# The pooled side one chunk ahead of the weighted sum, in the second weighted stage of a four-layer graph network

## The chip, the cores and the metric

The kernel runs on one core of one Trainium2 chip. The metric is the device time of one execution in microseconds. The kernel before took 19959.1 us (median of 3 runs, 19957.56 to 19962.43).

## The reference

Four residual graph layers over 12500 nodes with 64 features and 412500 directed edges, sorted by their target node. Each layer normalises x, applies a relu and adds one message passing step:

```python
h = jnp.maximum(_layernorm(x, axis=-1), 0.0)
x = x + _L0_gnn_ref(h, edge_weight1, src, dst, L0_gnn_W, L0_gnn_b)       # segment_sum(h[src] * e, dst) @ W.T + b
h = jnp.maximum(_layernorm(x, axis=-1), 0.0)
x = x + _L1_gnn_ref(h, edge_index, edge_attr_32, u, batch0, W1, b1, W2, b2)
h = jnp.maximum(_layernorm(x, axis=-1), 0.0)
x = x + _L2_gnn_ref(h, L2_gnn_weight_r, src, dst, edge_type_8)           # a relational layer over 8 types
h = jnp.maximum(_layernorm(x, axis=-1), 0.0)
x = x + _L3_gnn_ref(h, L3_gnn_attn_l, L3_gnn_attn_r, src, dst)           # a softmax attention layer

# inside _L1_gnn_ref, by source node (row = edge_index[0]):
seg_sum = jax.ops.segment_sum(edge_attr, row, num_segments=N)
seg_max = jax.ops.segment_max(edge_attr, row, num_segments=N)
cnt = jax.ops.segment_sum(jnp.ones((edge_attr.shape[0], 1)), row, num_segments=N)
h = jnp.concatenate([seg_sum, seg_max, seg_sum / jnp.maximum(cnt, 1.0), u[batch]], axis=1)
return jax.nn.relu(h @ W1 + b1) @ W2 + b2
```

The change touches the stage that computes the last two thirds of the weighted sum of layer 0 and, beside it, the sums and maxima of the edge features of layer 1 (the "pooled" work) and the count of edges per target node.

## The kernel before

**Tiling.** The edges are laid out as 128 partitions of J = 3224 edges. A chunk is L = 60 edges of every partition; there are 54. A segment sum is a running scan along each partition's edges with a link (0 or 1) that restarts it where the node changes; the scans are stored to HBM, and later one row per node, the last of its run, is fetched back.

**Stages, in order.** `gathered_layer("wsum", 0 .. 18)` (66 to 1825 us in the profile), `scatter_by_source`, which sorts the edge features by source node into `by_src` (to 7065), `gathered_layer("wsum", 18 .. 54, pooled=True)`, which is changed (to 10022), `first_layers`, which turns the fetched rows into the output of layers 0 and 1 (to 10479), then the relation gathers (to 14981), its update, the attention gathers (15291 to 19814) and its update. Between stages all engines meet at a barrier. The function `gathered_layer` is shared by all four gathered stages; what the change adds is bound to `pooled`, and `pooled` is true for this stage alone.

**The stage that is changed.** NC = 36 chunks, and for each chunk k three pieces of work on DVE:

- own(k), lines 555 to 618: waits for the chunk's gathered rows of h (`gathered`), multiplies them by the edge weights (line 580, which says `turned`) and scans them (line 616, `scanned`).
- count_side(k), lines 461 to 479: makes one-hots of 90 target indices (fewer in the last side) in HG = 3 groups of HL = 30, a `low` (line 478) and a `high` (line 479), in NB = 3 pairs of buffers. For each group it waits for `oh_used`, that is, for PE to have read what lies in the buffer; PE multiplies high by low, 30 matmuls a group (line 786), and so counts the edges per node.
- pool_side(k), lines 481 to 517: waits for 90 sorted rows (`prow_loaded`), for ACT to have turned them (`pturned`) and taken the side before (`ptaken`), and runs a sum scan and a max scan over them (line 511), which ends with `pscanned`.

The sides have 90 edges where a chunk has 60: the 36 sides cover all 54 chunks' edges, the 36 chunks only the last two thirds.

Around them:

- POOL, lines 430 to 446, gathers chunk k's rows of h, 60 indirect DMAs (line 437; 44 for the last chunk). Chunks 0 and 1 of the stage were gathered earlier. Before each chunk it waits for `index_ready` (ACT has copied the chunk's indices), `turned` (own(k-2) has used up the buffer) and `oh_used` (the count sides up to three before are on PE). Ahead of this it has the scatters of the sort, line 881. Behind the last gather it waits until all pooled scans are stored (line 453), and issues the first EARLY = 28 fetches of their rows (line 1066); first_layers issues the others.
- ACT, lines 689 to 757, for each k: `number_following(k)` (line 712) copies the indices of chunk k+2, once chunk k's rows have landed; `turn_pooled(k)` (line 692) turns the sorted rows of side k; own(k) (lines 737 and 739) turns and stores the chunk's scan; `take_pooled(k)` (lines 701 and 703) turns and stores the pooled scans in two halves through one buffer, so the second half waits until the first is stored.
- SP, lines 410 to 421: `load_rows(k)` loads the sorted rows of side k once side k-1 has been scanned (line 413); the first waits for the end of the scatters.

The order on each engine is the order in which the code is written; loops run over pairs of chunks with i = k // 2 and s = k % 2. DVE before: own, count, pool for k = 0 to 33, then own(34), pool(34), count(34), pool(35), count(35), own(35).

Of the kernel before, what the change touches and what calls it, by code (L numbers as in the profile page):

```python
# [43 lines left out]
def build(nc, x, src, dst, etype, weight, attr, W0, b0, u, W1, b1, W2, b2, Wr, attn_l, attn_r, out, L):  # L44
# [39 lines left out]
    with ctx:  # L84
# [204 lines left out]
        def gathered_layer(kind, table, width, rows_out, c0, c1, index, counts=None, pooled=False, weights=None,  # L289
# [5 lines left out]
            NC = c1 - c0  # L295
            SIDE = JP // NC
            SHORT = SIDE - (JP - J)
# [3 lines left out]
            CHUNKS = NC + (1 if REST else 0)  # L301
            rest_at = (NC - 1) * L + FINAL
            HG = SIDE // HL
            NB = HG
            BY, PBY = 512 // L, 512 // SIDE
            with ExitStack() as c:
# [151 lines left out]
                def _(dve):  # L458
# [158 lines left out]
                                                            ALU.mult, ALU.add)  # L617
                            last.then_inc(scanned, 1)

                    def side(i, s):  # L620

                        if counts:
                            count_side(i, s)
                        if pooled:
                            pool_side(i, s)

                    with dve.Fori(0, NC // 2 - 1) as i:
                        for s in range(2):
                            own(i, s)
                            side(i, s)  # L630
                    own(NC // 2 - 1, 0)
                    for s in range(2):
                        if pooled:
                            pool_side(NC // 2 - 1, s, SHORT if s else SIDE)
                        if counts:
                            count_side(NC // 2 - 1, s, SHORT if s else SIDE)
                    own(NC // 2 - 1, 1, FINAL)
# [36 lines left out]
                def _(act):  # L674
# [14 lines left out]
                    def turn_pooled(k, w=SIDE):  # L689

                        act.wait_ge(prow_loaded, 32 * k + 32)
                        nc.scalar.copy(by_feature_of(flat_of(pGf), A, w), prow[:, 1:w + 1, 0:A].rearrange("p j f -> p f j")).then_inc(pturned, 1)

                    def take_pooled(k, w=SIDE):

                        run = by_feature_of(flat_of(pSf), 2 * A, w)
                        act.wait_ge(pscanned, k + 2)
                        for half in range(2):
                            act.wait_ge(pstored, 32 * k + 16 * half + 16)
                            rows = slice(half * w // 2, (half + 1) * w // 2)  # L700
                            nc.scalar.copy(pS[:, 0:w // 2, :].rearrange("p j f -> p f j"), run[:, :, rows]).then_inc(ptaken, 1)  # L701
                            act.wait_ge(ptaken, 2 * k + half + 2)
                            act.dma_start(scan_pool[0:EP, :].rearrange("(p j) f -> p j f", p=P)[:, bass.ds(k * SIDE + half * w // 2, w // 2), :],
                                          pS[:, 0:w // 2, :]).then_inc(pstored, 16)
# [9 lines left out]
                    def own(i, s, w=L, following=True, at=None):  # L714
# [19 lines left out]
                            else:  # L734
# [3 lines left out]
                            act.wait_ge(taken_out, k + 2)  # L738
                            act.dma_start(rows_out[0:EP, :].rearrange("(p j) f -> p j f", p=P)[:, bass.ds(at, w), :],
                                          S[s][:, 0:w, :]).then_inc(stored[s], 16)  # L740
                    def own_and_pooled(i, s):

                        if pooled:
                            number_following(i, s)
                            turn_pooled(2 * i + s)
                        own(i, s)
                        if pooled:
                            take_pooled(2 * i + s)

                    with act.Fori(0, NC // 2 - 1) as i:  # L750
                        own_and_pooled(i, 0)
                        own_and_pooled(i, 1)
                    own_and_pooled(NC // 2 - 1, 0)
                    if pooled:
                        turn_pooled(NC - 1, SHORT)
                        take_pooled(NC - 1, SHORT)
                    own(NC // 2 - 1, 1, FINAL, False)
                    if REST:
                        own(NC // 2, 0, REST, False, rest_at)
# [891 lines left out]
        def attention_update():  # L1651
            with ExitStack() as c:  # L1652
# [61 lines left out]
                def _(sp):  # L1714
# [6 lines left out]
                    if N > full * P:  # L1721
# [9 lines left out]
                       pooled=True, weights=wt_all, carried=wsum_state)  # L1731
# [58 lines left out]
```

## Time and profile before

| | |
|---|---|
| median of 3 runs | 19959.1 us |
| profiled execution | 19961.19 us, its span 19959.5 us |
| POOL busy | 13577.9 us (68%) |
| DVE busy | 8460.5 us (42%) |
| ACT busy | 2726.7 us (14%) |
| PE busy | 2311.4 us (12%) |
| second weighted stage | 7065 to 10022 us |
| first_layers | 10022 to 10479 us |

The numbers come from one profiled execution. A line's busy time is the time in which its instructions were running on the engine; for an indirect DMA of POOL it is the time to issue it, not to carry it out. "Idle before" is the time for which the engine stood still ahead of an instruction, with what released it. "Issue" as a releaser means that nothing in the profile explains the pause. In a timeline ACTq and SPq are the issue of a transfer from that engine's queue. `wsum_C` is the count in PSUM, `lead_rows` the gathered rows, `H` in this stage the pooled scans, `wsum_idx` the indices that POOL reads, `taken` and `scan_wsum` belong to the correction that joins the partitions' runs in first_layers.

### The profile page before, as it was taken

What the parts mean: (1) busy time and instruction counts of PE and PEld (TensorE: products, weight loads), DVE (VectorE), ACT (ScalarE), POOL (GpSimd) and SP (SyncE); (2) the same over time, 40 slices, a digit from 0 to 9 for tenths busy, and PEclk for the clock granted to TensorE, in tenths of its full rate; (3) what the DMA queues carried; (4) which work ended last, traced back from release to release, by engine and by line L of the source; (5) the groups of instructions that cost most, each with busy time, mean ns of one, the idle gap of its engine ahead of it and who ended that gap; (6) DMA issues with size and microseconds to landing.
All of it is one profiled execution on the core that took longest, in us unless ns stands there. A gap on an engine that the chain in (4) does not pass through costs nothing. (4 is left out here: it accounts for less than half of the span.)

```text
span 19959.5 us, 67952 instructions
## 1 busy us (share of the span) xinstructions
PE 2311.4 (12%) x17213; PEld 2000.1 (10%) x17213; DVE 8460.5 (42%) x6902; ACT 2726.7 (14%) x1877; POOL 13577.9 (68%) x13406
## 2 busy tenths in 40 slices
PE   1112222222222211111140000000000000000000
PEld 1111222222222200000030000000000000000000
DVE  6666667766666666666631111111113222222222
ACT  0000010000100022222221111111110100111110
POOL 5665556665566666666637777777776777777776
PEclk7555555555555555555565555555555555555555
DMA  3111111111111122223321111111112111111111
GB/s 66 45 41 53 50 50 50 54 54 50 50 50 50 48 93 97 98 95 101 108 83 44 47 47 47 47 47 47 47 49 31 48 48 48 48 48 48 48 48 48
DMA packets 611147, 1134.47 MB, mean 57 GB/s; under 512 B 329487, under 2 KB 381168, under 8 KB 569104
## 3 DMA queue, kind: packets, MB, share of 16 engines
q0 software_dynamic: 428736, 387.04, 9.6%
q10 hardware_dynamic: 33984, 425.89, 5.2%
q1 hardware_dynamic: 148368, 320.87, 4.9%
q8 instruction: 22, 0.36, 0.0%
q14 instruction: 37, 0.30, 0.0%
HBM read 613.19 MB, written 519.73 MB: 57 GB/s over the span
## 5 line engine op out<-in xcount | busy, mean ns | idle before, releaser
L881 POOL DMA_INDIRECT by_src<-H,sort_place_i x3224 | 3131.1, 971 | 2047.9 <-DVE sort_place_i L949 1080.8
L437 POOL DMA_INDIRECT rel_G<-rel_table,rel_idx x3224 | 3457.0, 1072 | 1239.3 <-issue 1029.5
L437 POOL DMA_INDIRECT att_G<-att_table,att_idx x3224 | 3429.5, 1064 | 1057.9 <-issue 1057.9
L437 POOL DMA_INDIRECT lead_rows<-h_table,wsum_idx x3104 | 2948.5, 950 | 1581.8 <-issue 934.6
L610 DVE SCALAR_TENSOR_TENSOR rel_Gf<-rel_Sf,rel_keep_first,rel_Gf 128x64 f32<-128x64 f32 x55 | 18.5, 336 | 3964.7 <-ACT rel_Gf L729 2065.8
L584 DVE TENSOR_TENSOR_SCAN att_near<-att_near,er_in 128x60 f32<-128x60 f32 (+2 forms) x55 | 19.3, 351 | 3435.9 <-DMA att_G<-att_table,att_idx 3435.9
L1038 PE MATMUL pG<-sort_cnt,sort_lowT 128*128 128x98 f32 x6448 | 1273.8, 361 | 885.8 <-DVE sort_prod L935 819.5
L478 DVE TENSOR_TENSOR wsum_low<-iota_b,wsum_parts 128x3840 fp8e4<-128x3840 bf16 x216 | 891.8, 4129 | 1080.5 <-remote 881.4
L1038 PEld LDWEIGHTS pG<-sort_cnt,sort_lowT 128*128 128x128 f32 x6448 | 1155.7, 268 | 894.6 <-DVE sort_prod L935 827.5
L786 PE MATMUL wsum_C<-wsum_high,wsum_low 128*128 128x98 fp8e4 x6448 | 720.6, 267 | 3963.3 <-issue 3272.1
L935 DVE TENSOR_TENSOR sort_prod<-pG,sort_high 128x392 f32<-128x392 f32 x806 | 450.9, 565 | 1605.5 <-remote 1209.9
L989 ACT COPY sort_cnt<-pC 128x392 f32<-128x392 f32 x806 | 391.8, 486 | 4695.3 <-PE pC L1030 2300.9
L786 PEld LDWEIGHTS wsum_C<-wsum_high,wsum_low 128*128 128x128 fp8e4 x6448 | 526.0, 131 | 4158.0 <-issue 4157.6
L729 ACT COPY rel_Gf<-rel_G 128x3840 f32<-128x3840 f32 (+2 forms) x55 | 358.1, 6511 | 3293.6 <-DMA rel_G<-rel_table,rel_idx 3293.6
L928 DVE TENSOR_REDUCE sort_rank<-sort_keys 128x60 f32<-128x7680 int16 (+1 forms) x54 | 784.2, 14523 | 1.9
L920 DVE TENSOR_TENSOR sort_lowT<-sort_lows,sort_side 128x7680 f32<-128x7680 uint8 (+1 forms) x54 | 704.4, 13044 | 0.0
L1030 PE MATMUL pC<-sort_high,sort_low 128*128 128x98 bf16 x3224 | 354.9, 247 | 2932.8 <-DVE sort_lowT L920 1645.6
L479 DVE TENSOR_TENSOR wsum_high<-iota_b,wsum_parts 128x2940 fp8e4<-128x2940 bf16 x216 | 689.5, 3192 | 0.0
L701 ACT COPY pool_S<-H 128x2880 f32<-128x2880 f32 (+1 forms) x72 | 366.6, 5092 | 2083.8 <-DVE H L511 1700.8
L1030 PEld LDWEIGHTS pC<-sort_high,sort_low 128*128 128x128 bf16 x3224 | 299.0, 128 | 2974.6 <-issue 1896.5
L1289 PE MATMUL att_turn<-ident,att_tail 128*66 128x128 f32 x2 | 0.7, 450 | 4826.6 <-DMA sort_feat<-in_attr 4826.6
L737 ACT COPY att_S<-att_Sf 128x3840 f32<-128x3840 f32 (+2 forms) x55 | 397.3, 7223 | 918.4 <-issue 806.1
(357 smaller groups left out, 7398.5 us busy)
## 6 DMA issues: line engine op xcount, KB each, us to landing
scan_att<-att_S ACTq DMA_DIRECT2D x53, 1980.0 KB
scan_wsum<-wsum_S ACTq DMA_DIRECT2D x53, 1920.0 KB
sort_keys<-key_rows SPq DMA_DIRECT2D x53, 1920.0 KB
scan_rel<-rel_S ACTq DMA_DIRECT2D x53, 1920.0 KB
scan_pool<-pool_S ACTq DMA_DIRECT2D x70, 1440.0 KB
pool_row<-by_src SPq DMA_DIRECT2D x35, 1485.0 KB
by_src<-H,sort_place_i POOLq DMA_INDIRECT x3224
rel_G<-rel_table,rel_idx POOLq DMA_INDIRECT x3224
```

The lines of the kernel that those rows point to most:

```text
L437: pool.indirect_dma_start(out=G[s][:, j, :], out_offset=None, in_=table, in_offset=bass.IndirectOffsetOnAxis(ap=idx[s][:, j:j + 1], axis=0 ...
L478: v.tensor_tensor(low[b][:, 0:h, :], iota(P), part(0, P), ALU.is_equal, saturate=False)
L479: v.tensor_tensor(high[b][:, 0:h, :], iota(HT), part(1, HT), ALU.is_equal, saturate=False).then_inc(oh_ready, 1)
L737: nc.scalar.copy(S[s][:, 0:w, 0:D].rearrange("p j f -> p f j"), run).then_inc(taken_out, 1)
L786: last = mm(C[:, w * HT:(w + 1) * HT], low[g % NB][:, j, :], high[g % NB][:, j, :], start=False, stop=False, skip_group_check=True)
L881: pool.indirect_dma_start(out=by_src, out_offset=bass.IndirectOffsetOnAxis(ap=place_i[s][:, j:j + 1], axis=0), in_=row[s][:, j, :], in_off ...
L920: v.tensor_tensor(lowT[:, 0:n, :], lows[:, 0:P * n].rearrange("p (x j) -> p j x", j=n), own_near.unsqueeze(2).to_broadcast([P, n, P]), ALU ...
L928: v.tensor_reduce(rank[:, 0:n], keys[:, 0:P * n].rearrange("p (x j) -> p j x", j=n), AX, ALU.add).then_inc(ranked, 1)
L935: v.tensor_tensor(prod[n % 2][:], pG[n % 3][:, 0:W].rearrange("p (w h) -> p w h", w=WAYS), high[:, WAYS * g:WAYS * (g + 1), :], ALU.mult). ...
L989: a.copy(cnt[n % 2][:], pC[:, 0:W]).then_inc(snapped, 1)
L1030: last = mm(pC[:, w * HT:(w + 1) * HT], low[:, WAYS * g + w, :], high[:, WAYS * g + w, :], start=False, stop=False, skip_group_check=True)
L1038: last = mm(pG[n % 3][:, w * HT:(w + 1) * HT], lowT[:, WAYS * g + w, :], cnt[n % 2][:, w * HT:(w + 1) * HT], start=True, stop=True, skip_g ...
```

## The change

The pooled sides run one ahead of the chunks. DVE does own(0), pool(0), pool(1), count(0), own(1), pool(2), count(1), written out ahead of a loop that now begins with its second turn and does own(k), pool(k+1), count(k); the end is own(34), pool(35), count(34), count(35), own(35). The count sides keep their place between the own parts. On ACT, turn_pooled(0) and take_pooled(0) stand at the beginning, and each chunk's group then handles side k+1: number_following(k), turn_pooled(k+1), own(k), take_pooled(k+1). POOL, SP and PE are not changed. The other gathered stages keep their order.

```diff
--- before.py
+++ after.py
@@ -301,6 +301,7 @@
             CHUNKS = NC + (1 if REST else 0)
             rest_at = (NC - 1) * L + FINAL
             HG = SIDE // HL
+            AHEAD = 1 if pooled else 0
             NB = HG
             BY, PBY = 512 // L, 512 // SIDE
             with ExitStack() as c:
@@ -617,21 +618,25 @@
                                                             ALU.mult, ALU.add)
                             last.then_inc(scanned, 1)
 
-                    def side(i, s):
-
-                        if counts:
-                            count_side(i, s)
-                        if pooled:
-                            pool_side(i, s)
-
-                    with dve.Fori(0, NC // 2 - 1) as i:
+                    if AHEAD:
+                        own(0, 0)
+                        pool_side(0, 0)
+                        pool_side(0, 1)
+                        count_side(0, 0)
+                        own(0, 1)
+                        pool_side(0, 2)
+                        count_side(0, 1)
+                    with dve.Fori(AHEAD, NC // 2 - 1) as i:
                         for s in range(2):
                             own(i, s)
-                            side(i, s)
+                            if pooled:
+                                pool_side(i, s + AHEAD)
+                            if counts:
+                                count_side(i, s)
                     own(NC // 2 - 1, 0)
+                    if pooled:
+                        pool_side(NC // 2 - 1, 1, SHORT)
                     for s in range(2):
-                        if pooled:
-                            pool_side(NC // 2 - 1, s, SHORT if s else SIDE)
                         if counts:
                             count_side(NC // 2 - 1, s, SHORT if s else SIDE)
                     own(NC // 2 - 1, 1, FINAL)
@@ -738,22 +743,24 @@
                             act.wait_ge(taken_out, k + 2)
                             act.dma_start(rows_out[0:EP, :].rearrange("(p j) f -> p j f", p=P)[:, bass.ds(at, w), :],
                                           S[s][:, 0:w, :]).then_inc(stored[s], 16)
-                    def own_and_pooled(i, s):
+                    def own_and_pooled(i, s, k, w=SIDE):
 
                         if pooled:
                             number_following(i, s)
-                            turn_pooled(2 * i + s)
+                            turn_pooled(k, w)
                         own(i, s)
                         if pooled:
-                            take_pooled(2 * i + s)
-
-                    with act.Fori(0, NC // 2 - 1) as i:
-                        own_and_pooled(i, 0)
-                        own_and_pooled(i, 1)
-                    own_and_pooled(NC // 2 - 1, 0)
-                    if pooled:
-                        turn_pooled(NC - 1, SHORT)
-                        take_pooled(NC - 1, SHORT)
+                            take_pooled(k, w)
+
+                    if AHEAD:
+                        turn_pooled(0)
+                        take_pooled(0)
+                        for k in range(2):
+                            own_and_pooled(0, k, k + AHEAD)
+                    with act.Fori(AHEAD, NC // 2 - 1) as i:
+                        for s in range(2):
+                            own_and_pooled(i, s, 2 * i + (s + AHEAD))
+                    own_and_pooled(NC // 2 - 1, 0, NC - 1, SHORT)
                     own(NC // 2 - 1, 1, FINAL, False)
                     if REST:
                         own(NC // 2, 0, REST, False, rest_at)
```

On ACT, at the beginning of the stage, this stood before (line 712 copies the indices of the next chunk to be gathered, 692 turns sorted rows, 737 and 739 are own's copy and store, 701 and 703 the take):

```order
L750 ISA
L712 ISA [waits lead_gathered0]
L712 COPY wsum_idx<-src_all 128x60
L691 ISA
L692 COPY pool_Gf<-pool_row 128x2880 [waits wsum18_prow_loaded]
L735 ISA
L736 REGISTER_ALU [waits wsum18_stored1]
L737 COPY wsum_S<-wsum_Sf 128x64x60 [waits wsum18_scanned]
L739 ISA [waits wsum18_taken_out]
L739 DMA scan_wsum<-wsum_S 128x3840
L699 REGISTER_ALU [waits wsum18_pscanned]
```

And this stands there now (717 is the index copy, 697 the turn, 742 and 744 own, 706 and 708 the take):

```order
L697 COPY pool_Gf<-pool_row 128x2880 [waits wsum18_prow_loaded]
L706 COPY pool_S<-H 128x64x45 [waits wsum18_pstored,wsum18_pscanned]
L708 DMA scan_pool<-pool_S 128x2880 [waits wsum18_ptaken]
L706 COPY pool_S<-H 128x64x45 [waits wsum18_pstored]
L708 DMA scan_pool<-pool_S 128x2880 [waits wsum18_ptaken]
L717 COPY wsum_idx<-src_all 128x60 [waits lead_gathered0]
L697 COPY pool_Gf<-pool_row 128x2880 [waits wsum18_prow_loaded]
L742 COPY wsum_S<-wsum_Sf 128x64x60 [waits wsum18_scanned,wsum18_stored1]
L744 DMA scan_wsum<-wsum_S 128x3840 [waits wsum18_taken_out]
```

The first index copy moved behind the turn and the take of side 0.

On DVE, at the end of the stage, the last pooled side (lines 489 to 511) stood behind the last one-hots of count side 34 (lines 478 and 479):

```order
L478 TENSOR_TENSOR wsum_low<-iota_b,wsum_parts 128x3840 [waits wsum18_onehot_used]
L479 TENSOR_TENSOR wsum_high<-iota_b,wsum_parts 128x2940
L478 TENSOR_TENSOR wsum_low<-iota_b,wsum_parts 128x3840 [waits wsum18_onehot_used]
L479 TENSOR_TENSOR wsum_high<-iota_b,wsum_parts 128x2940
L489 MEMSET pool_same 128x5 [waits wsum18_pscanned,wsum18_prow_loaded]
L490 MEMSET pool_cut 128x5
L491 TENSOR_TENSOR pool_first<-pool_row 128x1
L492 TENSOR_TENSOR pool_same<-pool_row 128x5x73
L495 TENSOR_SCALAR pool_first<-pool_first 128x1 [waits wsum18_psame_ready]
L496 TENSOR_SCALAR pool_cut<-pool_same 128x5x73
L504 SCALAR_TENSOR_TENSOR pool_Gf<-pool_state,pool_first,pool_row 128x32 [waits wsum18_ptaken,wsum18_pstate_ready,wsum18_pturned,wsum18_pcut_ready]
```

Now it (lines 490 to 512) stands directly behind the scans of own(34) (line 617), ahead of count sides 34 and 35:

```order
L617 SCALAR_TENSOR_TENSOR wsum_Sf<-wsum_wide,wsum_Gf 128x480 [waits wsum18_taken_out,wsum18_begun]
L617 SCALAR_TENSOR_TENSOR wsum_Sf<-wsum_wide,wsum_Gf 128x480 x7
L490 MEMSET pool_same 128x5 [waits wsum18_pscanned,wsum18_prow_loaded]
L491 MEMSET pool_cut 128x5
L492 TENSOR_TENSOR pool_first<-pool_row 128x1
L493 TENSOR_TENSOR pool_same<-pool_row 128x5x73
L496 TENSOR_SCALAR pool_first<-pool_first 128x1 [waits wsum18_psame_ready]
L497 TENSOR_SCALAR pool_cut<-pool_same 128x5x73
L505 SCALAR_TENSOR_TENSOR pool_Gf<-pool_state,pool_first,pool_row 128x32 [waits wsum18_ptaken,wsum18_pstate_ready,wsum18_pturned,wsum18_pcut_ready]
```

So between the last pooled side and the last own part there are two count sides now, where there was one.

## Rows read from the trace of the kernel before

**Rows 1.** Windows: interval, length, busy of PE, PEld, DVE, ACT, POOL, clock, DMA.

```profile
7065.00:10022.00 2957.00, 395.62 (x3230) 277.88 (x3230) 1940.37 (x1569) 799.20 (x179) 1952.03 (x2055) 0.51 0.30 101
10022.00:10479.00 457.00, 207.52 (x1067) 143.88 (x1067) 123.75 (x286) 92.87 (x168) 181.10 (x181) 0.68 0.27 81
10479.00:14981.00 4502.00, 1.37 (x4) 0.78 (x4) 520.87 (x615) 725.11 (x165) 3457.04 (x3224) 0.50 0.17 47
```

**Rows 2.** Waits of POOL in the stage: waited for, us in total, times, longest.

```profile
POOL lead_rows L437 <- PE wsum_C L786: 325.1, 22, 20.7
```

**Rows 3.** Windows of L437: interval, length, POOL busy (gathers), clock, DMA.

```profile
8443.00:8528.20 85.20, 57.25 (x61) 0.50 0.29 99
8528.20:8698.60 170.40, 113.87 (x121) 0.50 0.30 99
```

**Rows 4.** Windows of L786 alone: interval, length, PE busy (matmuls), PEld busy.

```profile
8441.30:8445.00 3.70, 3.39 (x40) 3.17 (x40) 0.50 0.04 8
8460.00:8520.00 60.00, 3.87 (x22) 2.02 (x22) 0.50 0.38 133
```

**Rows 5.** Timeline of ACT: start, us, line, operation [idle before <-releaser].

```profile
7065.62 0.24 ACT L712 COPY wsum_idx<-src_all 128x60 int32 x1 [46.36 <-PEq L811]
7087.96 5.34 ACT L692 COPY pool_Gf<-pool_row 128x2880 f32<-128x2880 f32 x1 [22.10 <-DMA pool_row<-by_src]
```

**Rows 6.** Timeline of POOL, its first gather of the stage.

```profile
7080.18 0.98 POOL L437 DMA_INDIRECT lead_rows<-h_table,wsum_idx  x1 [0.30 <-issue]
```

**Rows 7.** Timeline of DVE: a one-hot, then a pooled side's beginning.

```profile
8527.54 4.15 DVE L478 TENSOR_TENSOR wsum_low<-iota_b,wsum_parts 128x3840 fp8e4<-128x3840 bf16 x1 [24.11 <-remote]
...
8534.74 0.15 DVE L491 TENSOR_TENSOR pool_first<-pool_row 128x1 f32<-128x1 f32 x1
...
8536.69 0.28 DVE L504 SCALAR_TENSOR_TENSOR pool_Gf<-pool_state,pool_first,pool_row 128x32 f32<-128x32 f32 x1 [0.21 <-DVE pool_cut L496]
```

**Rows 8.** Timeline of ACT: take_pooled, then the next index copy.

```profile
8550.35 5.16 ACT L701 COPY pool_S<-H 128x2880 f32<-128x2880 f32 x1 [50.54 <-DVE H L511]
...
8566.89 0.24 ACT L712 COPY wsum_idx<-src_all 128x60 int32 x1 [0.97 <-ACT pool_S L701]
```

**Rows 9.** Timeline of POOL and DVE: last gather of chunk 19, then own(19).

```profile
8602.37 0.95 POOL L437 DMA_INDIRECT lead_rows<-h_table,wsum_idx  x1 [0.30 <-issue]
...
8605.98 0.16 DVE L568 TENSOR_TENSOR wsum_keep_first<-dst_all 128x1 f32 x1
```

**Rows 10.** Timeline of POOL: last gather, first early fetch.

```profile
9937.46 0.95 POOL L437 DMA_INDIRECT lead_rows<-h_table,wsum_idx  x1 [0.30 <-issue]
9998.98 0.95 POOL L1066 DMA_INDIRECT H<-scan_pool,end_src  x1 [60.58 <-DMA scan_pool<-pool_S]
```

**Rows 11.** Timeline of DVE, the stage's end.

```profile
9953.49 4.15 DVE L478 TENSOR_TENSOR wsum_low<-iota_b,wsum_parts 128x3840 fp8e4<-128x3840 bf16 x1 [11.14 <-remote]
...
9967.91 0.19 DVE L491 TENSOR_TENSOR pool_first<-pool_row 128x1 f32<-128x1 f32 x1
...
9981.04 0.19 DVE L465 TENSOR_SCALAR wsum_parts_i<-dst_all 128x74 int32<-128x74 int32 x1
...
10012.05 0.23 DVE L647 COPY count_dst<-wsum_C 128x98 f32<-128x98 f32 x1
```

**Rows 12.** Timeline of SP, its first transfer of first_layers.

```profile
10063.75 5.60 SPq L1099 DMA_DIRECT2D pool_edge_keys<-by_src  x4
```

**Rows 13.** Timeline of POOL in first_layers: the correction, the last fetch.

```profile
10133.31 1.64 POOL L1298 DMA_INDIRECT scan_wsum<-taken,fix_row  x1 [14.43 <-DVE taken L1277]
...
10270.41 0.95 POOL L1066 DMA_INDIRECT V_wsum<-scan_wsum,end_dst  x1 [0.30 <-issue]
```

**Rows 14.** Timeline of ACT in first_layers.

```profile
10160.05 1.01 ACT L1462 ACTIVATE hid<-pH,b_hid 128x896 f32<-128x896 f32 x1 [8.05 <-issue]
...
10286.49 1.01 ACT L1462 ACTIVATE hid<-pH,b_hid 128x896 f32<-128x896 f32 x1 [46.12 <-remote]
```

**Rows 15.** DMA queue: packets, MB, share.

```profile
q14 instruction: 37, 0.30, 0.0%
```

## The prediction

> **What bounds the kernel now.** I read the windows by stage first. The change touches one stage, the second weighted one, 7065 to 10022 us, and through its end the next one, first_layers. In that stage POOL is busy 1952 of 2957 us and DVE 1940; in the relation stage POOL is busy 3457 of 4502 us, DVE 521 [rows 1]. Neither share names a bound by itself, so I next read POOL's waits. Its gathers wait 325.1 us in 22 waits for PE's counting matmuls [rows 2]. At first sight PE, or the DVE that makes its one-hots, is what holds POOL.
>
> The gathers by window say more. A chunk of 60 takes 85.2 us, in the rows where POOL paused 9.9 us and where it did not: 85.2 us for one, 170.4 for two [rows 3]. PE by window shows two paces: 40 matmuls in 3.7 us just before a burst, 22 matmuls in 60 us within it, 2.7 us each, with almost no busy time [rows 4]. So PE is not short of work, it is held up while gathers are in flight, and it holds POOL only because it is held. In the relation stage, which has no matmuls to wait for, 3224 gathers take 4502 us, 1.40 us each or 83.8 us per 60 [rows 1]; here it is 85.2. I take it that the gathers need about 1.4 us each downstream of POOL, which issues one in 1.25 us, and that the waits on PE are where POOL gives the difference back. The chunk is then set by gathers, and own work, pooled side and count side lie beside it (DVE's 1940 us over 36 chunks are 54 us out of 85), whatever their order.
>
> **The start (+44 us).** Before, ACT copies the indices of chunk 2 at once, at 7065.6, and POOL's first gather follows its last scatter with 0.30 us idle at 7080.18 [rows 5, 6]. After, that copy stands behind turn_pooled(0) and take_pooled(0) on ACT. The first waits for the sorted rows and starts at 7087.96, after 22.1 us idle, and takes 5.34 us: 7093.3. Then DVE's pooled scans, which wait for it: the DVE chain from its first state instruction at 8536.69 to ACT's copy at 8550.35 is 13.7 us [rows 7, 8]: 7107.0. DVE is free by then, since own(0) alone stands ahead. ACT's take has two copies and the landing of a store between them, 8550.35 to the index copy at 8566.89, 16.5 us [rows 8]: 7123.5. First gather about 7124.3, 44 us later, with POOL idle. Nothing hides it, because gathers pace the stage. Ends: if the extra room at the start lets PE and DVE get ahead, part is made up, down to 0; if the second index copy, behind take_pooled(1), is late as well, another 20: 0 to +64.
>
> **The loop (0 us).** Removed: nothing. On DVE the pooled side of chunk k+1 now stands between own(k) and count(k). Between two count sides there is one own and one pooled side either way, so count sides come at the same distance. What moves is own(k): it follows count(k-1) directly, 16 us earlier in the cycle (a pooled side begins at 8534.74 and ACT copies its result at 8550.35 [rows 7, 8]). Before, own(19) starts at 8605.98, 3.6 us after POOL issued the last gather that it needs, at 8602.37 [rows 9], which is about when it has landed. So after the change it waits for its gathers there, up to 16 us, and pool and count queue behind it. That wait falls in the time in which DVE waits for PE anyway, since the one-hot buffers are three and PE is held (24.11 us before one of them [rows 7]), so I price it at 0. Bounds: the stage's pace against the relation stage's, 85.2 - 83.8 = 1.4 us per chunk to win over 33 chunks (-46); and, if a third of the 16 us isn't covered in every third chunk, 1.8 per chunk (+59). ACT's turn, own and take, and SP's row load, which waits for the scans of the side before, move one side ahead with the same counts, and have 85 us for 35 us of work.
>
> **The end of the stage (+22 us beside the start).** Before: last gather issued 9937.46, and PE lets DVE go on at 9953.49 after 11.1 us idle [rows 10, 11]. Then two one-hot pairs to 9967.91, the last pooled side to 9981.04 (13.1 us), count side and own part to 10012.05, stores and end at 10022. POOL meanwhile waits 60.6 us for the last take's store, until 9998.98 [rows 10], and then issues 28 early fetches at 1.25 us, to 10034. After, the last pooled side comes right behind own(34), so it leaves this tail: -13.1. But its take lands before the gathers end, so POOL issues its 28 early fetches right behind them, 35 us more without a pause. If they hold up PE as gathers do, the release of 15 to 16 us after the last issue comes 35 us later. Sum -13.1 + 35 = +22. Ends: -13 (fetches hold nobody up) and +27 (PE takes 5 us longer to recover after so long a burst). I take +22, since PE's pace in rows 4 is tied to POOL's issuing and not to which table is read.
>
> **first_layers (-11 us).** Before, POOL still issues early fetches when the stage ends, and SP's first transfer leaves only at 10063.75, 41 us after 10022 [rows 12]; POOL's next step, the correction at 10133.31, waits 14.43 us for DVE's result of that chain [rows 13], 111 us after the stage's end. After, POOL has nothing left to issue at that moment, so SP is quick, and the correction is bound by POOL's own 66 fetches up to it: 66 x 1.26 = 84 us after the stage's end. That is -27. Against it: before, the pause of 14.4 us let PE and ACT run; ACT's steps are 12 us apart around 10160 and then none starts freely till 10286.49, 15 us after POOL's last fetch at 10270.41 [rows 13, 14]. Without that pause one group more is left for the end, about +10, and recovery after 150 fetches in a row may take 5 to 6 us more. -27 + 10 + 6 = -11. Ends -27 and +15.
>
> **Sum.** 44 + 0 + 22 - 11 = +55 us on the profiled execution's 19961.2; the median of the runs is 19959.1, 2 us less, so 20014. The relation and attention stages are not touched.
>
> **A rule weighed.** The instruction queue q14 moved 37 packets in the whole execution [rows 15], so no loop is fetched anew in each turn. The Trainium skill (Runtime: NRT & Kernel Launch, Instruction fetch mechanics) says that the sequencer refills instruction memory in blocks of 256 instructions through a DMA queue of its own, and that a taken branch out of the loaded window stalls. The trace agrees that the loops stay inside. By that rule the chunks now written out ahead of the loop would cost one block more on DVE, hidden or a few us; the sum is made without it.
>
> **Rivals.**
> (a) The start is made up, no change. Gathers have slack after all: DVE and PE enter the loop with more count sides done, POOL skips early waits (each up to 20.7 us), and the early fetches don't hold up PE. Of the 44, 30 are recovered, the end gives -13 and first_layers -11: -10, or 19949; from -36, with -27 behind, to +20. For it: POOL does pause for PE in 22 places. Against: the 85.2 us is the same with and without a pause.
> (b) Faster: POOL's waits on PE are real and the new order removes them, because DVE is ready with one-hots sooner. The stage at the issue rate would save 325 us; at the relation stage's pace 46 us. With the start's 44 and the rest's +11, even the latter is +9, so (b) needs more than 95 of the 325 us to be faster by 40. If half goes: 44 + 11 - 163 = -108, 19851. For it: the waits' row. Against: the relation stage waits for no PE and is hardly quicker.
> (c) Slower by more, by one mechanism: own(k) on DVE waits for its gathers with pool(k+1) and count(k) queued behind, one-hots come late, PE gets them only after POOL has started again, and POOL then waits for a whole extra release. The place is the third chunk of each pattern, the price 5 us or more per three chunks, 11 times: +55 on top, 20070; it decides from the point where own's wait exceeds the 24 us for which DVE waits for PE now [rows 7]. Less of it is +20.
> (d) The pooled side does not come earlier in effect (SP's load waits for the same scans): then only the start's +44 stays and the end is as before, 20003. It counts with the forecast.
>
> **Chances.** Forecast with (d) 0.54, (a) 0.21, (b) 0.12, (c) 0.13. What a measurement can tell from no change is 0.2%, 40 us. The forecast's own spread, 19985 to 20045, lies mostly above 19999, a tenth of it below. So faster 0.13, same 0.25, slower 0.62. Range 19940 to 20075: it takes in most of (a) and of (c), leaves out (b) and the far ends of both.
>
> **What would show it.** In the profile after: the first L437 gather at about 7124 with its idle put down to ACT's index copy; the second stage's chunks still 85 us apart; POOL's waits on PE near 325 us again; the first early fetch directly behind the last gather; the first release of PE some 50 us after the last gather of chunk 35; SP's first transfer of first_layers a few us after the stage's end. Wrong would be: a gather period below 84 us (b), above 86.5 (c), or a stage that ends less than 25 us later although the first gather is 44 later (a).

## The result and the profile after

| | before | after |
|---|---|---|
| median (22 runs each, same chip) | 19958.33 us | 20003.73 us |
| lowest to highest | 19933.06 to 19978.06 | 19972.43 to 20021.43 |
| profiled execution's span | 19959.5 us | 20011.1 us |

The ratio is 1.0021 with a 95% interval of 1.0014 to 1.0028: the change costs 45 us, 28 to 56 by the interval. The forecast was 55 us. (Every ratio here is the one on record for the comparison; it can differ from the quotient of the two medians by up to 0.0006.)

The profile after, group by group. POOL's waits from 7065 to 10100 us, in the columns of [rows 2]:

```profile
POOL lead_rows L438 <- PE wsum_C L793: 320.6, 22, 20.1
POOL lead_rows L438 <- ACT wsum_idx L717: 43.2, 1, 43.2
```

The 22 waits for PE are still there, with 320.6 us where they had 325.1. New is one wait of 43.2 us for ACT's index copy. The timelines of ACT and POOL at the beginning of the stage show it, against [rows 5, 6]:

```profile
7102.46 5.31 ACT L697 COPY pool_Gf<-pool_row 128x2880 f32<-128x2880 f32 x1 [68.32 <-DMA pool_row<-by_src]
...
7136.85 0.24 ACT L717 COPY wsum_idx<-src_all 128x60 int32<-128x60 int32 x1 [0.41 <-ACT pool_S L706]
```

```profile
7093.82 0.97 POOL L888 DMA_INDIRECT by_src<-H,sort_place_i  x1 [0.30 <-issue]
7137.99 0.98 POOL L438 DMA_INDIRECT lead_rows<-h_table,wsum_idx  x1 [43.20 <-ACT wsum_idx L717]
```

The last scatter is at 7093.82 here and at 7078.90 before: the stages ahead of the change took 15 us longer in this execution. Nothing in them was changed, and across this study the end of the sort moved by as much as 83 us between kernels that ran on one chip with the same code up to there (6944.8 to 7027.5), and to 7085.5 in a later comparison under the same chip's number. So spans of single profiles don't compare; from here on I count from the last scatter, in four stretches: to the first gather, from first to last gather, from the last gather to DVE's copy of the counts (the last row of [rows 11]), and from there to the first gather of the relation stage.

DVE's waits in the stage (7080 to 10103), same columns:

```profile
DVE wsum_low L479 <- remote: 810.2, 31, 47.4
DVE wsum_near L579 <- DMA lead_rows<-h_table,wsum_idx: 162.3, 11, 14.9
```

Own(k) now waits for its gathered rows 11 times, up to 14.9 us, as worked out from [rows 9]. In return DVE's idle time ahead of line 479, its wait for one-hot buffers, is 861 us in all, where it was 968. The loop is no slower: from the first gather of POOL's seventh burst to that of its thirty-first a chunk takes 85.1 us here and 85.2 before, and first to last gather is 2853.3 us here and 2857.3 before.

The end of the stage, POOL and DVE, against [rows 10, 11]:

```profile
9991.28 0.94 POOL L438 DMA_INDIRECT lead_rows<-h_table,wsum_idx  x1 [0.30 <-issue]
9992.53 0.94 POOL L1073 DMA_INDIRECT H<-scan_pool,end_src  x1 [0.30 <-issue]
```

```profile
10047.36 4.15 DVE L479 TENSOR_TENSOR wsum_low<-iota_b,wsum_parts 128x3840 fp8e4<-128x3840 bf16 x1 [47.39 <-remote]
...
10092.77 0.23 DVE L652 COPY count_dst<-wsum_C 128x98 f32<-128x98 f32 x1
```

The early fetches follow the last gather without a pause. PE lets DVE go on 56.1 us after the last gather (10047.36 - 9991.28), where it was 16.0 us before, and the whole stretch is 101.5 us instead of 74.6.

In first_layers, SP, POOL and ACT, against [rows 12 to 14]:

```profile
10105.06 1.76 SPq L1106 DMA_DIRECT2D pool_edge_keys<-by_src  x4
```

```profile
10197.80 1.64 POOL L1305 DMA_INDIRECT scan_wsum<-taken,fix_row  x1 [0.30 <-issue]
...
10325.96 1.02 POOL L1073 DMA_INDIRECT V_wsum<-scan_wsum,end_dst  x1 [0.30 <-issue]
```

```profile
10334.49 1.01 ACT L1469 ACTIVATE hid<-pH,b_hid 128x896 f32<-128x896 f32 x1 [89.39 <-remote]
```

SP is quick: 12.3 us after the counts' copy instead of 51.7. The correction no longer waits for DVE, POOL's own fetches bind it; it comes 105.0 us after the counts' copy, where it was 121.3. ACT resumes 8.5 us after POOL's last fetch, where it took 16 before. Three of ACT's steps of this line got through ahead of that, at 10181, 10187 and 10225, as many as before (10148, 10160 and 10220). This stretch is 437.6 us, 31.4 less than before.

### The profile page after: what moved, and what is told of

Same layout as the page of the kernel before. It is cut to its first block and busy times, and to the rows that moved or that the text cites. A ratio compares the mean times of both kernels' runs of the same rounds, so it can differ in the third digit from the quotient of the medians.

```text
span 20011.1 us, 67931 instructions
## 1 busy us (share of the span) xinstructions
PE 2303.3 (12%) x17213; PEld 1993.1 (10%) x17213; DVE 8454.0 (42%) x6902; ACT 2728.5 (14%) x1877; POOL 13566.6 (68%) x13406
## 5 line engine op out<-in xcount | busy, mean ns | idle before, releaser
L742 ACT COPY wsum_S<-wsum_Sf 128x3840 f32<-128x3840 f32 (+1 forms) x54 | 362.4, 6711 | 1445.5 <-DVE wsum_Sf L617 1275.6
```

Source lines behind the costliest of these rows:

```text
L742: nc.scalar.copy(S[s][:, 0:w, 0:D].rearrange("p j f -> p f j"), run).then_inc(taken_out, 1)
```

## The experiments

Twelve kernels ran, in four comparisons, each with the kernel before timed beside it. The stretches below are in us, each from one profile. The kernel before has one profile only, from the first comparison, and the pace differs a little between comparisons: a chunk in the loop takes 85.2 us in it, 84.9 in e1, e2, e3, e6, e6b and e7, and 85.4 in e10. The 0.3 us make some 10 us over the stage, so those six compare best with each other.

| | to first gather | gathers | to the counts' copy | to the relation stage | sum |
|---|---|---|---|---|---|
| before | 1.3 | 2857.3 | 74.6 | 469.0 | 3402.2 |
| after | 44.2 | 2853.3 | 101.5 | 437.6 | 3436.5 |
| e1_index_first | 1.3 | 2864.8 | 77.6 | 444.3 | 3387.9 |
| e2_old_end | 44.1 | 2846.9 | 75.5 | 469.1 | 3435.6 |
| e3_fetch_after_counts | 44.2 | 2843.7 | 61.9 | 469.9 | 3419.7 |
| e7_index_first_fetch_late | 1.3 | 2865.0 | 48.5 | 472.2 | 3387.0 |
| e10_start_as_before | 1.3 | 2873.2 | 78.3 | 445.3 | 3398.1 |
| e6b_spread_more | 1.3 | 2861.4 | 38.3 | 469.9 | 3370.9 |

**The index copy in its old place.** The changed kernel, with this on ACT (an extract):

```diff
                     if AHEAD:
+                        number_following(0, 0)
                         turn_pooled(0)
                         take_pooled(0)
                         for k in range(2):
-                            own_and_pooled(0, k, k + AHEAD)
+                            own_and_pooled(0, k, k + AHEAD, number=k > 0)
```

> The changed kernel, with one move undone: on ACT the first index copy (number_following(0)) stands again ahead of the turn and the take of side 0. Theory: the start costs 43 us of POOL idle that nothing gives back, because gathers pace the stage. Then the first gather follows the last scatter with 0.3 us idle again. POOL's second burst may wait some 8 us longer than in the kernel before, since own(1) now stands behind two pooled sides and a count side and says 'turned' only about 93 us after the first gather. So 43 - 8 = 35 us come back, 19968, within 10 us of the kernel before. Rival a (the start was made up inside the stage): less than 15 us come back, 19990 or more, and the last gather is issued as long after the sort's end as in the changed kernel.

Measured: 19883.9 us against 19895.43, ratio 1.0000, interval 0.9991 to 1.0009. With it the changed kernel's loss is gone, as far as an interval of 18 us to each side tells. POOL's new wait in its gathers:

```profile
POOL lead_rows L438 <- DVE wsum_Gf L581: 17.4, 1, 17.4
```

The second burst waits 17.4 us for own(1), which says `turned` only behind two pooled sides and a count side, and the gathers' stretch is 7.5 us longer than before, as expected. Against e2, which ran in the same comparison with the late start, it is 18 us longer. So of the 43 us some 25 come back at the last gather. The other large part is the end of the stage: 77.6 us and not 101.5, with the early fetches issued as early as in the changed kernel. PE lets DVE go on 47.4 us after the last gather, not much sooner than the 56.1 of the changed kernel, but behind that DVE has three pairs of one-hots left to make and not five. So the 27 us there are not the fetches alone; where the end falls in the pattern of three chunks has a part in it.

**The old end on DVE.**

```diff
                     own(NC // 2 - 1, 0)
-                    if pooled:
-                        pool_side(NC // 2 - 1, 1, SHORT)
                     for s in range(2):
+                        if pooled and s:
+                            pool_side(NC // 2 - 1, 1, SHORT)
                         if counts:
```

> The changed kernel with the end of the second weighted stage undone on DVE: count side 34, then the last pooled side, then count side 35, as before. ACT and POOL are the changed ones. Theory of the prediction: the early fetches go back behind the take of the last side, about 60 us after the last gather; PE is released 15 to 16 us after the last gather; the stage ends 22 us earlier than in the changed kernel, and first_layers takes about 11 us more by the forecast, but about 31 more by the trace of the changed kernel. So 19993 by the forecast's sizes, 20013 by the trace's. If early fetches hold nobody up, the stage would end 13 us later than in the changed kernel instead.

Measured: 19928.51 against 19895.43, 1.0018, 1.0009 to 1.0028. This has the start's loss and nothing else: 44.1, then 75.5 and 469.1 like the kernel before. By the profiles it is equal to the changed kernel (3435.6 and 3436.5): the changed end costs 26 us and gives 31 back, and the rest is the pace of the loop in the two comparisons.

**The early fetches behind the counts.**

```diff
                         pool.wait_ge(pstate_ready, NC + 1)
+                        pool.wait_ge(counted, 1)
                         fetch(pool, scan_pool, end_src, H, 1, range(EARLY))
```

> The changed kernel, where POOL waits for the end of the counting matmuls before it issues the 28 early fetches. Theory: the early fetches, issued right behind the gathers, are what holds PE and with it DVE for 35 us longer. Without them PE is released 15 to 16 us after the last gather instead of 55, the last pooled side no longer lies in the tail, and the stage ends 35 to 39 us earlier than in the changed kernel. POOL then still issues at the stage's end, so SP's first transfer of first_layers is 40 us late again and first_layers takes 25 to 35 us more: 19995 in all. Rival (PE is slow for another reason, such as the long burst of gathers before): PE is released as late as in the changed kernel, and the time is 20030.

Measured: 19921.57 against 19895.43, 1.0012, 1.0003 to 1.0021. POOL's last gather and first early fetch, and DVE's release:

```profile
9901.55 0.94 POOL L438 DMA_INDIRECT lead_rows<-h_table,wsum_idx  x1 [0.30 <-issue]
9953.54 0.94 POOL L1074 DMA_INDIRECT H<-scan_pool,end_src  x1 [51.05 <-PE wsum_C L803]
```

```profile
9918.08 4.15 DVE L480 TENSOR_TENSOR wsum_low<-iota_b,wsum_parts 128x3840 fp8e4<-128x3840 bf16 x1 [20.87 <-remote]
```

The release is 16.5 us after the last gather again, and the stretch is 61.9: 12.7 less than before, against the 13.1 of a pooled side. This shows both halves of the end's term. First_layers is back at 469.9. The early fetches alone, then, make the end 39.6 us longer (101.5 against 61.9) and first_layers 32.3 us shorter.

**No wait on PE.** The kernel before, where POOL's `wait_ge(oh_used, ...)` is left out of the pooled stage.

> The kernel before, where POOL's gathers of the second weighted stage no longer wait for the counting matmuls (the buffers that they fill don't depend on them). Theory (gathers need about 1.4 us each downstream of POOL, the waits only give back what POOL is ahead): POOL's waits on PE go, waits of another kind take their place or each gather is issued later, and a chunk still takes 83 to 86 us; PE gets no pauses to run in and DVE falls behind with the count sides, which may make it slower by up to 100 us. 19950 to 20060. Rival b (the waits on PE are the bound): chunks of 75 us, 325 us less, 19640.

Measured: 20431.29 against 19895.43, 1.0270, 1.0256 to 1.0284. Both theories missed the size. POOL's waits:

```profile
POOL lead_rows L437 <- ACT wsum_idx L712: 800.6, 16, 57.9
```

A pair of chunks takes 199 us on average, not 170. POOL issues two bursts back to back and then waits some 50 us for the next indices. Those stand on ACT behind the take of the side before, that side stands on DVE behind a count side, and DVE's waits for one-hot buffers grew: those put down to "remote" from 773 to 1363 us. Taking the 325 us of waits away brings no gain here, but a longer wait has come in their place, so this run alone doesn't put rival (b) out; the next two do. Why it is more than my theory said is a reading that no run tests: the wait makes POOL pause where PE needs the pause, and in this order of DVE without it the whole ring stalls longer. PE fits that: 34 of its 108 groups of one-hots took over 40 us, where 19 did before.

**No counts at all.** The kernel before without count sides, their matmuls and POOL's wait for them in this stage.

> The kernel before, with the count sides, their matmuls and POOL's wait for them left out of the second weighted stage (the counts per target node come out as zero). It shows the pace of the gathers alone. Theory (gathers need about 1.4 us each downstream of POOL): a chunk of 60 still takes 84 us, as in the relation stage, the stage is some 45 us shorter and POOL gets pauses of another kind. Rival b (PE's release is what sets 85 us): a chunk takes 75 us, POOL's issue rate, and the stage is about 330 us shorter.

Measured: 19794.58 against 19831.23, 0.9982, 0.9972 to 0.9991. The window of two chunks, and POOL's line 437 over the stage (columns: busy us, mean ns | idle before):

```profile
8007.50:8175.50 168.00, 126.61 (x120) 0.50 0.31 100
```

```profile
L437 POOL DMA_INDIRECT lead_rows<-h_table,wsum_idx x2024 | 2114.2, 1045 | 688.4 <-issue 688.4
```

84.0 us a chunk, without a single wait for another engine in POOL's gathers, and one gather takes 1045 ns to issue instead of 950. First to last gather is 2801.2 us, 56 less than before. The counts' work hides behind the gathers but for those 56 us. (The total moved less than the stage: first_layers took 17 us more and what follows it 52. With counts of zero many of the later fetches read one and the same row; that this is the reason is not tested.)

**Spreading the gathers.** A one-column memset on POOL ahead of every second gather, and ahead of every one (an extract; the semaphore waits that go with it are left out).

```diff
                         for j in range(w):
+                            if pooled and j % 2 == 0:      # second kernel: every j
+                                nc.gpsimd.memset(pause[:, j:j + 1], 0.0).then_inc(paused, 1)
                             pool.indirect_dma_start(
```

> The kernel before, with a one-column memset on POOL ahead of every second gather of the second weighted stage, so that a gather is issued every 1.40 us on average and not every 1.25. Theory (PE is held while POOL is ahead of what the gathers take downstream): PE is held less, the 20 and 10 us pauses of POOL shrink or go, a chunk takes 84 to 87 us and the time stays within 0.3% of the kernel before. Rival (PE is held whenever any gather is in flight): PE is held as long as before or longer, pauses of 10 us per chunk stay and come on top, 94 us a chunk, 300 us slower.

> The same with a memset ahead of every gather: 1.55 us apart, 93 us a chunk. This is slower by about 270 us in either case; what it tells is PE. Theory: POOL is never ahead, so PE's 30 matmuls of a group always take under 10 us, and POOL never waits for PE. Rival (held by any gather in flight): groups of 60 us and more and waits of POOL on PE remain.

Measured: 19831.15 and 19822.67 against 19831.23, 0.9997 (0.9987 to 1.0006) and 0.9992 (0.9983 to 1.0001). As a way to slow POOL it failed: the memset takes 0.11 us inside the 0.30 us that lie between two gathers anyway, so most stayed 1.25 us apart. The first kernel's time came as expected, but not for the reason given; the 270 us expected of the second didn't come; and the question about PE stays open. With a memset ahead of each gather PE was held in more places and for shorter: 69 of its 108 groups took over 5 us, 8 of them over 40 (45 and 19 before), which neither side had expected. But it told something better. POOL's waits with a memset ahead of each gather:

```profile
POOL lead_rows L443 <- issue: 608.3, 1982, 2.2
POOL pause L442 <- remote: 58.6, 31, 3.9
...
POOL pause L442 <- PE wsum_C L795: 3.3, 1, 3.3
```

The pauses of 10 and 20 us are gone, and the gathers' stretch stayed (2861.4). What POOL waits at the beginning of a chunk went from 325 us to 62: 3.3 us put down to PE, and 58.6 in 31 waits for which the trace names no engine ("remote"), none over 3.9 us. In their place single gathers are issued up to 2.2 us late. The row with the 325 us was never worth 325 us. The end of the stage is 36 us shorter in this profile: DVE had no wait for PE left behind the last gather. The times show at most 34 us of that (0.9983) and may show none, and the profile is of the slowest of the ten runs.

**Index copy first, fetches late.** Both mends together.

> The changed kernel with the first index copy in its old place and the early fetches behind the end of the counting matmuls. From the parts: the start as in the kernel before but 8 us for own(1) behind two pooled sides; PE released 15 to 20 us after the last gather; the last pooled side out of the tail, -13; POOL still issuing at the stage's end, so first_layers as in the kernel before. In all -5 against the kernel before, ratio 0.9998; against the version with the index copy alone mended, about +10.

Measured: 19810.9 against 19831.23, 0.9992, 0.9983 to 1.0001. By stretches it equals the one with the index copy alone (3387.0 and 3387.9), where I had expected 10 us more. The fetches behind the counts make the end 29.1 us shorter and first_layers 27.9 us longer.

**Three kernels on a chip where gathers don't back up.** This comparison fell on another chip, on which the kernel before takes 17032.82 us (27 runs, 17027.65 to 17041.45). The first is the kernel before with `EARLY = 0`; the second and third are e1 and e7 with the memsets.

> The kernel before, with none of the 28 early fetches in the second weighted stage: first_layers issues them itself. Theory: what made first_layers 31 us shorter in the changed kernel is, first, that POOL is idle at the stage's end, so that SP's first transfer leaves 2 us after it instead of 41, and second, that the 28 fetches (35 us of POOL) are done by then. Here only the first holds. The stage ends as before; SP is quick; the correction waits for POOL's fetches and comes some 20 us later than before; first_layers takes 5 to 10 us more than before. 0 to +10 us, ratio 1.0000 to 1.0005. Rival (idle POOL alone shortens it): first_layers 25 us shorter, ratio 0.9988.

> The changed kernel with the index copy in its old place and a one-column memset ahead of each gather. From the parts: the version with the index copy alone was 14 us shorter than the kernel before by its stages, the memsets alone 31 us, most of it because PE is released sooner behind the last gather. If both add up, 45 us less than before, ratio 0.9978. If the 31 us belonged to the place in the pattern of three chunks at which the stage happens to end, it comes out between 0.9985 and 1.0000.

> The same, with the early fetches behind the end of the counting matmuls. The stage ends sooner by up to 13 us, first_layers takes 25 to 30 us more: 10 to 15 us slower than the version without this, ratio 0.9985.

Measured: 1.0014 (1.0005 to 1.0023), 1.0006 (0.9997 to 1.0015) and 1.0014 (1.0005 to 1.0023). Against the kernel before all three are slower than expected, the first at the edge of its interval. The expectations were worked out for 85 us a chunk, and since the kernel before has no profile there, a split against it is not to be had. The first is 24 us slower by the medians, though SP's first transfer left 12.2 us after the counts' copy as expected, so the rival, that an idle POOL alone makes it faster by 0.12%, is out here. Between the second and the third it is 14.5 us by the medians, 10 to 15 expected, but the parts were others: the stage's end is the same (29.7 us both), and first_layers is 11.8 us longer instead of 25 to 30. The number was luck. The changed kernel itself did not run on this chip. What the first shows is the machine. POOL's gathers by window, in this stage and in the relation stage, and the waits of the whole chip in this stage:

```profile
5662.80:8152.00 2489.20, 1884.65 (x1984) 0.50 0.34 115
8561.00:12600.00 4039.00, 3048.89 (x3220) 0.50 0.18 52
```

```profile
PE wsum_C L786 <- DVE wsum_high L479: 2284.7, 105, 73.7
...
POOL lead_rows L437 <- issue: 616.9, 2024, 0.3
```

A gather takes 1.25 us in both stages, 75 us a chunk, with the same program. No wait of POOL on PE is left. PE waits for DVE alone, and none of its groups of 30 matmuls takes 5 us, where some 45 of 107 took longer in the first profile. In this stage PE's hold-up and the gathers' 1.40 us come and go together.

**The old start.** The changed kernel, which puts the pooled sides ahead only in chunk 1.

```diff
                         own(0, 0)
-                        pool_side(0, 0)
-                        pool_side(0, 1)
                         count_side(0, 0)
+                        pool_side(0, 0)
                         own(0, 1)
+                        pool_side(0, 1)
                         pool_side(0, 2)
                         count_side(0, 1)
```

with ACT doing chunks 0 and 1 as before, then turn_pooled(2) and take_pooled(2).

> The changed kernel with the start of the kernel before: own(0), count(0), pool(0), own(1), pool(1), and only then the second pooled side that puts them one ahead, pool(2), count(1); ACT and the index copies likewise. Theory from the stages of the other runs: no pause of POOL at the start (43 us back) and none of the 8 to 19 us for a late own(1); the end of the stage between 3 and 27 us longer than in the kernel before where gathers pace it, 13 to 18 us shorter where POOL's issue does; first_layers 25 to 31 us shorter. So where a chunk takes 85 us: 0 to 25 us less than the kernel before, ratio 0.9987 to 1.0000; where it takes 75 us, 25 to 45 us less, ratio 0.9974 to 0.9985. If the start was not the whole of the changed kernel's loss, it is above 1.0000.

Measured: 19978.35 against 19998.94, 0.9991, 0.9982 to 1.0000, with a chunk at 85 us. The start's pause is gone. Whether it is faster than the kernel before isn't settled: the interval ends at 1, and the profile has only 4 us between them. Its gathers' stretch is 16 us longer than before, for which the expectation had nothing; some 5 are the pace of this comparison, and the rest isn't explained.

## Why the prediction was right

**The bound.** Right, and shown. Gathers alone take 84.0 us a chunk (no counts), the waits ahead of a chunk can shrink from 325 us to 62 without a gain (memsets), and removing them by force made it slower. The counts still cost 56 us over the stage, about 1.6 us a chunk; I had named 46 as the most there was to win there. The difference is that I divided the whole relation stage, 4502 us; from its first to its last gather it takes 4486 us, 83.5 per 60.

**The start, +44.** Measured 42.9 (44.2 against 1.3), and putting one instruction back takes POOL's pause away. The pause hides something, though: with it own(1) is never late, and without it POOL waits 17.4 us there. Nothing in the stage gave the 43 us back but 4 us in the gathers' stretch, which is within what that stretch varies between kernels that differ only behind it (2843.7 to 2853.3).

**The loop, 0.** Measured -4, or 0.1 us a chunk. The wait of own(k) for its rows came as predicted, 14.9 us in every third chunk, and DVE's wait for one-hot buffers covered it, which shrank by 107 us.

**The end, +22.** Measured +26.9. The parts are shown: 12.7 of 13.1 for the pooled side, and the early fetches for the rest: 56.1 us to the release instead of 16, so 40 us where I took 35. The whole term isn't a constant. In the kernel with the index copy mended it is 3 us; the fetches still cost 29.1 us there (77.6 against 48.5), but without them that kernel's end would be 26 us shorter than before and not 13, by where it falls in the pattern of three chunks.

**first_layers, -11.** This is the term that was mis-sized: it measured -31.4. SP's delay went as said (-39). The correction came only 16 us earlier and not 27, since the 66 fetches ahead of it took 93.5 us, 1.42 us each, where I reckoned 1.26. The 102 fetches behind it then took 128.2 us instead of 137.1, so the last of them is 25 us earlier, near my 27 by another way. The losses that I set against it, +10 for a missing pause and +6 for a longer recovery, did not come: as many of ACT's steps got through as before, without a pause of POOL, and ACT resumed 8.5 us after the last fetch and not 16 or more, another 8 us. The profiles in which the fetches stand right behind the gathers (after, e1, e10) have 437.6 to 445.3 us, and the others 468 to 472, but for the one without counts. Why PE could run I can't explain further: from 10172 to 10193 it worked with hardly a break while POOL fetched without one, though 28 of the same fetches behind a burst of gathers held it, and behind 10193 it was held again.

**The sum.** By stretches 34 us, by the medians 45 with 28 to 56 as its interval, forecast 55. The error of 20 us in first_layers is most of the difference to the profile. The rest of the two spans' difference of 51.6 us is 15 us ahead of the change and 2 behind it. So the medians' nearness to the forecast, 45 against 55, is in part luck; what the trace bears out is 34. Of the written-out chunks, whose loading I priced at nothing, no run shows a cost: q14 moved 38 packets against 37 before, and 38 as well in the kernel without counts, which has no chunk written out ahead of the loop.

**The rivals.** (a), the start made up in the stage: it isn't, by the start's mend. Its last part, -27 in first_layers, did come. (b), POOL's waits as the bound: out, by the kernel without counts and by the memsets. (c), own's wait not covered: the wait came and was covered. (d), the pooled side not early in effect: out, the take had landed when the gathers ended. That its 20003 is the measured median to the microsecond is chance: the end cost 27 us and first_layers gave back 31.

## What to carry to other kernels

When work is moved ahead of a loop, look at what each engine does in its first turn: here one 0.24 us copy behind a turn and a take left the pacing engine idle for 43 us, ten times what the new order in the loop moved. A large wait of the busiest engine need not be a price: ask whether the same work takes the same time in a stage that has nothing to wait for, and only the excess can be won. And work that is issued early, at the end of a stage, can cost that stage about as much as it saves the next one: here 29 to 40 us against 28 to 32. Look at both before you count either.

## What the hardware showed

- The same program took 19831 to 19999 us in four comparisons and 17033 us in one, on another chip. 19831 and 19999 are from two comparisons under one chip's number, so a part of the drift is not the chip. In the profiles on the quick chip the relation stage's 3224 gathers took 4031 to 4035 us instead of 4486, 1.25 us each instead of 1.39, and the sort's last scatter came at 5653 to 5662 us instead of 7079.
- Where gathers back up, PE is held while they are in flight (2.7 us a matmul against 0.09 us), and on the quick chip, where they don't, it is not (no group of 30 over 2.6 us). What ties the two is open; the attempt to slow POOL below the gathers' own pace failed, since the memset hid in POOL's gap.
- A memset of 0.11 us between two gathers of POOL costs next to nothing: on the quick chip a chunk of 60 takes 75.9 us with them and 75.3 without.
